# A recommendation tower on one core: three table looks replaced by six gathers, and a repack read over three queues

## The reference

```python
e = jnp.stack([tbl_0[ids[:, 0]], ..., tbl_25[ids[:, 25]]], axis=1)        # 2048 x 26 x 128
combined = jnp.concatenate([dense[:, None, :], e], axis=1)                # 27 features
interactions = jnp.einsum('bnd,bmd->bnm', combined, combined)[:, _TRIU_I, _TRIU_J]
h = jnp.concatenate([dense, interactions, dense], axis=1)
h = jnp.maximum(h @ W_top1 + b_top1, 0.0)                                 # 607 -> 512
h = jnp.maximum(h @ W_top2 + b_top2, 0.0)                                 # 512 -> 256
y = h @ W_top3                                                            # 256 -> 1
```

## Time and profile before

| | |
|---|---|
| median of 3 runs | 382.11 us (381.92 to 382.95) |
| profiled execution | 382.7 us, span 380.8 us |
| PE busy | 343.5 us, 90% |
| PEld busy | 306.4 us, 80% |
| POOL busy | 251.5 us, 66% |
| DVE busy | 193.3 us, 51% |
| ACT busy | 125.4 us, 33% |
| chain that ended last | PE 79%, DVE 12%, issue 4%, DMA 3%, ACT 1%, POOL 1% |
| DMA | 44.32 MB, mean 116 GB/s |

### The profile page before, as it was taken

The page is one execution under the profiler, slowest core; times in us unless marked ns, Lnnn a source line. Parts: engine busy times, 40 slices in busy tenths (PEclk is TensorE's granted clock), DMA queues, the critical chain, the costliest instruction groups (busy, mean ns, idle before and its releaser), DMA issues.

```text
span 380.8 us, 13111 instructions
## 1 busy us (share of the span) xinstructions
PE 343.5 (90%) x6048; PEld 306.4 (80%) x6048; DVE 193.3 (51%) x94; ACT 125.4 (33%) x211; POOL 251.5 (66%) x267
## 2 busy tenths in 40 slices
PE   0888878679999999999999999999999999999995
PEld 0878767579888898888988898889888898887763
DVE  3899995329733395228833395228733495200000
ACT  2343433214322342324322442324322343434122
POOL 4777887777777777777777777777777777600200
PEclk9999999759999999999999999999999999999999
DMA  8766534935522534235522535235522533331400
GB/s 207 166 177 167 137 93 142 278 104 183 131 76 58 189 91 124 58 86 173 134 72 53 194 84 131 58 112 152 134 63 59 188 88 79 125 93 29 158 8 0
DMA packets 31156, 44.32 MB, mean 116 GB/s; under 512 B 17659, under 2 KB 23043, under 8 KB 31102
## 3 DMA queue, kind: packets, MB, share of 16 engines
q1 hardware_dynamic: 22494, 26.44, 23.0%
q0 software_dynamic: 8320, 16.92, 17.3%
q10 hardware_dynamic: 288, 0.13, 0.2%
HBM read 32.97 MB, written 10.49 MB: 114 GB/s over the span
## 4 chain that ended last, share of the span: by engine, by line
PE 79%; DVE 12%; issue 4%; DMA 3%; ACT 1%; POOL 1%; SPq 0%; DVEq 0%
PE look_ps L317 34%; PE mid_ps L347 13%; PE layer_ps L364 11%; DVE match L472 9%; PE layer_ps L373 7%; PE mid_ps L329 7%; PE layer_ps L361 4%; DVE table_low L480 3%; DMA rows<-in_table,index 2%; PE layer_ps L380 2%; DMA look_ids<-in_look_rows 1%; POOL rows L298 1%; ACT hidden L539 0%; ACT hidden L545 0%; ACT turned L512 0%
## 5 line engine op out<-in xcount | busy, mean ns | idle before, releaser
L298 POOL DMA_INDIRECT rows<-in_table,index x256 | 248.3, 970 | 81.6 <-issue 75.6
L472 DVE TENSOR_TENSOR match<-look_ids,row_number_ps 125x2048 fp32r<-125x2048 int16 x80 | 181.8, 2285 | 129.3 <-PE look_ps L317 122.8
L317 PE MATMUL look_ps<-match,table_high 125*128 125x256 f32 x640 | 166.2, 297 | 19.3 <-DVE table_low L480 17.0
L317 PE MATMUL look_ps<-match,table_low 125*128 125x256 f32 x640 | 159.7, 287 | 2.9 <-issue 2.9
L317 PEld LDWEIGHTS look_ps<-match,table_high 125*128 125x128 f32 x640 | 124.8, 195 | 27.5 <-issue 18.1
L317 PEld LDWEIGHTS look_ps<-match,table_low 125*128 125x128 f32 x640 | 125.2, 196 | 0.0
L347 PEld LDWEIGHTS mid_ps<-turned 128*32 128x32 f32 x4096 | 46.8, 111 | 22.0 <-issue 19.0
L347 PE MATMUL mid_ps<-turned 128*32 128x27 f32 x4096 | 55.2, 198 | 8.8 <-issue 4.9
L512 ACT COPY turned<-look_ps 128x512 f32<-128x512 f32 x40 | 32.0, 799 | 74.8 <-PE look_ps L317 74.8
L364 PE MATMUL layer_ps<-pairs,w_pairs_sb 117*128 117x256 f32 x192 | 46.7, 378 | 0.0
L519 ACT COPY turned<-mid_ps 128x512 f32<-128x512 f32 x64 | 42.8, 672 | 11.3 <-PE mid_ps L329 10.8
(11 more groups left out here) (21 smaller groups left out, 44.8 us busy)
## 6 DMA issues: line engine op xcount, KB each, us to landing
scratch<-grams SPq DMA_DIRECT2D x8, 864.0 KB, 4.6
look_ids<-in_look_rows SPq DMA_DIRECT2D x40, 128.0 KB, 4.1
rows<-in_table,index POOLq DMA_INDIRECT x256
scratch<-grams SPq DMA_DIRECT2D x8, 416.0 KB, 5.8
pairs<-scratch SPq DMA_DIRECT2D x92, 29.2 KB
grams<-in_table SPq DMA_DIRECT2D x4, 448.0 KB
pairs<-in_table SPq DMA_DIRECT2D x3, 448.0 KB
hidden<-in_table SPq DMA_DIRECT2D x3, 448.0 KB
```

Source lines behind the costliest of these rows:

```text
L298: pool.indirect_dma_start(out=rows[j % 2][:, at, :], out_offset=None, in_=tables[GATHERED[at]], in_offset=bass.IndirectOffsetOnAxis(ap=ind ...
L317: last = nc.tensor.matmul(look_ps[pair % 2][:, r % 2, :], part[0:table_rows, r, c, :], match[number % 2][0:table_rows, c, :], start=(c == ...
L472: nc.vector.tensor_tensor(match[number % 2][0:table_rows], look_ids[b][0:table_rows, r % 2].unsqueeze(1).broadcast_to(shape), row_number_p ...
```

## The change

`EXTRA = (0, 1, 2)`: in these groups table 23, the tenth looked one, is not looked but gathered, into a tile of its own, `extra` (128 samples x 2 tiles x 128). `index` gets a 17th column with its ids.

- POOL issues two more gathers behind the 16 of tiles 0, 2 and 4. They wait for the whole index (first time) and for the last `turn_extra` (the others).
- PE has `turn_extra(g)`, two transposes into a `mid_ps` bank, in place of look(g, 9): behind look(0, 6) in group 0, behind turn(g, 3) in groups 1 and 2.
- The DVE makes no match for them. In the opening split_low(9) comes right behind split_low(8), in front of matches(1, 6) to (1, 8).
- ACT's copy of the fifth pair takes one look in those groups, and `take_extra` copies the two transposes.
- Numbers of looks, pairs and of the `mid_ps` steps come from lists written out in order.
- The last repack's middle chunk is issued by ACT, between relu1(6) and relu2(6), with a semaphore of its own.

```diff
+EXTRA = (0, 1, 2)
+COLUMNS = len(GATHERED) + 1
...
+        def looks_of(g):
+            return LOOKS - 1 if g in EXTRA else LOOKS
...
+        def mid_order():
+            yield from (("turn", 0, k) for k in range(5))
+            yield "extra", 0, 0
+            yield from (("turn", 0, k) for k in range(5, TURNS))
+            for g in range(1, groups):
+                for k in range(STEPS):
+                    yield "gram", g - 1, k
+                    yield "turn", g, k
+                if g in EXTRA:
+                    yield "extra", g, 0
+                if g + 1 < groups:
+                    yield from (("turn", g, k) for k in range(STEPS, TURNS))
...
-                for c in range(CHUNKS if g + 1 < groups else CHUNKS - 1):
+                for c in range(CHUNKS if g + 1 < groups else 1):
                     load_pairs(sp, g, c, pairs_in)
...
+                g = j // TILES
+                if j % TILES == 0 and g in EXTRA:
+                    if j == 0:
+                        pool.wait_ge(index_in, 16)
+                    after(pool, extra_turned, EXTRA.index(g))
+                    for t in range(TILES):
+                        pool.indirect_dma_start(
+                            out=extra[:, t, :], out_offset=None, in_=tables[LOOKED[LOOKS - 1]],
+                            in_offset=bass.IndirectOffsetOnAxis(ap=index[:, j + t, COLUMNS - 1:COLUMNS], axis=0),
+                        ).then_inc(extra_in, 16)
...
+            def turn_extra(g):
+                number = extra_number(g)
+                after(pe, mid_out, number - 2)
+                pe.wait_ge(extra_in, 16 * TILES * (EXTRA.index(g) + 1))
+                for t in range(TILES):
+                    last = nc.tensor.transpose(mid_ps[number % 3][:, t * P:(t + 1) * P], extra[:, t, :], identity[:])
+                last.then_inc(extra_turned, 1)
...
             look(0, 6)
+            turn_extra(0)
+            look(0, 7)
             turn(0, 5)
-            look(0, 7)
+            look(0, 8)
             turn(0, 6)
-            look(0, 8)
             turn(0, 7)
-            look(0, 9)
...
                 turn(g, 3)
-                look(g, 9)
+                if g in EXTRA:
+                    turn_extra(g)
+                else:
+                    look(g, 9)
...
-            for r in range(LOOKS):
+            for r in range(looks_of(0)):
                 matches(0, r)
                 split_low(r)
                 if r < AHEAD:
                     matches(1, r)
-            for r in range(AHEAD, LOOKS):
+            split_low(LOOKS - 1)
+            for r in range(AHEAD, looks_of(1)):
                 matches(1, r)
...
             for g in (groups - 2, groups - 1):
                 for half in range(2):
                     relu1(g, half)
+                if g + 2 == groups:
+                    act.wait_ge(scratch_in, SCRATCH_DMAS * groups)
+                    act.wait_ge(layer1_done, 2 * (groups - 2))
+                    load_pairs(act, groups - 1, 1, middle_chunk_in)
                 relu2(g)
                 copy_y(g)
```

More of the change, by code:

```diff
@@ L72, in build @@
         rows = [sbuf(f"rows{b}", [P, len(GATHERED), D]) for b in range(2)]
-        index = sbuf("index", [P, groups * TILES, len(GATHERED)], int32)
+        extra = sbuf("extra", [P, TILES, D])
+        index = sbuf("index", [P, groups * TILES, COLUMNS], int32)
         grams = sbuf("grams", [P, FEATURES, IN_QUAD])
@@ L109, in build @@
         gathered = [[sem(f"gathered{b}_{u}") for u in range(UNITS)] for b in range(2)]
+        extra_in = sem("extra_in")
+        extra_turned = sem("extra_turned")
         zeroed = sem("zeroed")
@@ L126, in build @@
         pairs_in = sem("pairs_in")
+        middle_chunk_in = sem("middle_chunk_in")
         last_chunk_in = sem("last_chunk_in")
@@ L142, in after, with look_order @@
                 eng.wait_ge(sem, count)
-        def look_number(g, r):
[L146 to L150, removed]
+        def looks_of(g):
+            return LOOKS - 1 if g in EXTRA else LOOKS
+        def look_order():
+            yield from ((g, r) for r in range(AHEAD) for g in (0, 1))
+            yield from ((g, r) for g in (0, 1) for r in range(AHEAD, looks_of(g)))
+            yield from ((g, r) for g in range(2, groups) for r in range(looks_of(g)))
+        look_place = {look: number for number, look in enumerate(look_order())}
+        def look_number(g, r):
+            return look_place[g, r]
         def pair_number(g, q):
@@ L157, in pair_number, with extra_number @@
             return LOOK_PAIRS * g + q
+        pair_place = {pair_number(g, q): (g, q) for g in range(groups) for q in range(LOOK_PAIRS)}
         def pair_end(number):
[L161 to L168, removed]
-        def turn_number(g, k):
[L171 to L176, removed]
+            g, q = pair_place[number]
+            return look_number(g, min(2 * q + 1, looks_of(g) - 1)) + 1
+        def mid_order():
[10 more added lines that the diff above has]
+                    yield from (("turn", g, k) for k in range(STEPS, TURNS))
+            yield from (("gram", g, 0), ("gram", g, 1))
+            yield from (("turn", g, k) for k in range(STEPS, TURNS))
+            yield from (("gram", g, 2), ("gram", g, 3))
+        mid_place = {step: number for number, step in enumerate(mid_order())}
+        def turn_number(g, k):
+            return mid_place["turn", g, k]
         def gram_number(g, k):
[L179 to L182, removed]
+            return mid_place["gram", g, k]
+        def extra_number(g):
+            return mid_place["extra", g, 0]
         block = ctx.enter_context(nc.Block())
@@ L498, in _ @@
             for g in range(2, groups):
-                for r in range(LOOKS):
+                for r in range(looks_of(g)):
                     matches(g, r)
@@ L511, in take_look, with take_extra @@
                 act.wait_ge(look_done, pair_end(number))
-                nc.scalar.copy(by_sample[g % 2][:, :, 1 + 2 * pair:3 + 2 * pair],
-                               look_ps[number % 2][:].rearrange("d f n -> d n f")).then_inc(looked, 1)
+                n = min(2, looks_of(g) - 2 * pair)
+                nc.scalar.copy(by_sample[g % 2][:, :, 1 + 2 * pair:1 + 2 * pair + n],
+                               look_ps[number % 2][:, 0:n].rearrange("d f n -> d n f")).then_inc(looked, 1)
+            def take_extra(g):
+                act.wait_ge(extra_turned, EXTRA.index(g) + 1)
+                nc.scalar.copy(by_sample[g % 2][:, :, LOOKS], mid_ps[extra_number(g) % 3][:, 0:N]).then_inc(mid_out, 1)
             def take_turned(g, k):
@@ L552, in copy_y @@
                 nc.scalar.copy(y_row[:, g % 2, :], layer_ps[1][0:1, 0, :]).then_inc(y_copied, 1)
-            nc.scalar.dma_start(index[:, 0], index_t[:, 0:len(GATHERED)]).then_inc(first_index_in, 16)
+            nc.scalar.dma_start(index[:, 0], index_t[:, 0:COLUMNS]).then_inc(first_index_in, 16)
             nc.scalar.dma_start(index[:, 1:].rearrange("p a b -> p (a b)"),
-                                index_t[:, len(GATHERED):]).then_inc(index_in, 16)
+                                index_t[:, COLUMNS:]).then_inc(index_in, 16)
             for r in range(RAWS):
@@ L566, in _ @@
             split_high(9)
+            take_extra(0)
+            take_look(0, 3)
             take_turned(0, 5)
-            take_look(0, 3)
             take_turned(0, 6)
+            take_look(0, 4)
             take_turned(0, 7)
-            take_look(0, 4)
             act.wait_ge(dense_in, 16)
@@ L594, in _ @@
                 take_turned(g, 3)
+                if g in EXTRA:
+                    take_extra(g)
                 take_look(g, 4)
@@ L659 @@
     w1_pairs = w1[order].reshape(CHUNKS, CHUNK_ROWS, H1).transpose(1, 0, 2)
-    index = a["ids"][:, GATHERED].reshape(batch // P, P, len(GATHERED)).transpose(1, 0, 2).reshape(P, -1)
+    index = a["ids"][:, GATHERED + LOOKED[-1:]].reshape(batch // P, P, COLUMNS).transpose(1, 0, 2).reshape(P, -1)
     low_halves = np.ascontiguousarray(a["ids"]).view(np.int16).reshape(batch, TABLES, -1)[:, :, 0]
```

5 lines of the change are left out of this document (3 added, 2 removed).

## The result

The changed kernel takes 385.05 us (median of 15 runs, 383.81 to 386.25) against 382.44 us for the kernel before beside it. The ratio is 1.0063 with a 95% interval of 1.0044 to 1.0082, so it is 1.7 to 3.1 us slower; 383.7 was forecast. One of the 15 executions of the kernel before took 639.39 us and is left out of the ratio. The profiled execution took 383.81 us, the fastest of the 15, with a span of 381.8 us (380.8 before). Its difference to the profile before, 1.1 us, is therefore smaller than that of the medians, 2.6 us.

What follows compares the result with a forecast made beforehand. POOL's gather row was taken as full, pinning a full PE: 2.8 us late at gather 64, 1.6 given back, 1.75 late at gather 96, hence +1.6: 384.3 us profiled, 383.7 median (own range 382.6 to 385.3; overall 381.3 to 387.0).

Steps and rivals of the forecast that it cites:

- Price of a look: On PE in groups 0 to 2: each look replaced by two transposes saves 1.6 us, 4.8 us in all if unhindered.
- Pin at gather 64: Last gather of group 1: its turn waits until 98.2 us against 95.46 before, so PE is 2.8 us late.
- Pin at gather 96: Last gather of group 2: its turn waits until 140.7 us against 138.95 before, 1.75 us late.
- Gather 40: In the opening: its turn at 65.7 us against 65.52 before, up to 71.0 if it meets the bulk load.
- The sum: Whole kernel: lateness from group 2 is carried to the end, +1.6 us, 384.3 us profiled, 383.7 for the median.
- Rival A: TensorE's clock falls in PE's new waits at gathers 40 and 64: +4.7 us, 386.8 us; chance 0.17.
- Rival B: Fewer opening gathers collide with DVE splits, each avoided moving both pins 0.75 us forward: 382.2 us or below; chance 0.15.
- Tail: Last repack's middle chunk moved from SP to ACT: 0 us, ends 0 and +0.8 us.
- T: Experiments' theory: POOL's full gather row pins PE at gathers 64, 96; gave extra_1 +0.4 us, extra_2 1.6 faster, extra_4_5 3.2 faster.

Runs made afterwards that it cites:

- gathers_beside: The kernel before with the six gathers added into a tile that nobody reads, all looks kept, old tail; ratio 1.0100 to the kernel before.
- no_gathers: The changed kernel with the old tail and without its six gathers, PE transposing zeros instead; ratio 0.9898 to the kernel before.
- gathers_old_tail: The changed kernel without its tail part, the last repack read over two queues again; ratio 1.0085 to the kernel before.
- tail_alone: The kernel before with only the tail part, ACT issuing the last repack's middle chunk; ratio 1.0018 to the kernel before.
- extra_1: The changed kernel with old tail and old opening order, table 23 gathered in group 1 alone; ratio 1.0057 to the kernel before.
- extra_2: The changed kernel with old tail and old opening order, table 23 gathered in group 2 alone; ratio 1.0001 to the kernel before.
- extra_4_5: The changed kernel with old tail and old opening order, table 23 gathered in groups 4 and 5; ratio 0.9998 to the kernel before.
- late_none: The kernel before with group 7's last four turns moved behind layer2(5), no gathers added; ratio 1.0076 to the kernel before.

## Why the prediction was right, and where it was off

The direction and the mechanism held. POOL's 66% was a full row. The six added gathers pushed its end from 330.48 to 337.09 us, which is 6 x 1.25 less one collision, and PE's saved looks turned into waits, among them those at the two gathers named. The chain runs through POOL up to gather 64, and gathers_beside and no_gathers show the same cost from both sides.

Not all of it held. The waits for rows came to 10.7 us where 3 to 8 were forecast, and the longest, 4.43 us at gather 52, is one for which the prediction listed no margin. It cost nothing of its own, because gather 64 pins PE behind it. The median lies 1.35 us above the forecast one, near the upper end of its own range (385.3), and the interval of the difference begins at 1.7 us, just above the forecast 1.6: the place was better predicted than the size.

- **Price of a look (1.6 us)**: 1.69 us in the profiles.
- **Pin at gather 64 (98.2 us)**: 98.97. The gather itself started at 94.84 in place of 95.7, a collision fewer, and its landing took 4.13 us to the turn, not 2.5. The two errors went against each other, which is luck. In gathers_old_tail the landing was 2.70.
- **Pin at gather 96 (140.7 us)**: 139.93, from 137.29 and a landing of 2.64.
- **Gather 40 (65.7 to 71.0 us)**: 69.07. It met the bulk load, as the upper end assumed; the turn of gather 64 made that lateness unimportant.
- **The sum (+1.6 us)**: +2.6 us in the medians, 1.7 to 3.1. In the profile PE was 1.0 us late at gather 96, 0.4 us early by group 6, and 1.0 us late at the end; in gathers_old_tail 1.3 us late at gather 96 and 2.2 at the last turn. That the profile ends as late as it was at gather 96 is luck too: PE had made the lateness good by group 6 and lost it again in group 7, in a pause of 0.73 us at 325.33 and in gram(7, 0), 2.16 us instead of 1.49. A term that the sum did not have is PE's own pauses, which I took as the same in both programs. They are not: they come at other places in each. No run shows how much of the missing 1 us they are.
- **Rival A (clock)**: its mechanism is there, but it does not set this profile's time. Time at 1.2 GHz is (1 - clock) x 2 x length: before 13.4 us in one stretch from 70 to 84; after 3.5 + 3.6 + 6.4 = 13.5 us in three pieces. Two of the three belong to waits for rows: behind the 3.20 us at gather 40 the clock was at 0.50 or 0.51 from 70 to 73 us, and in the 4.43 us at gather 52 it fell and stayed at 0.50 from 84 to 90. Both lie ahead of gather 64, where the chain is POOL's, so they delay nothing. The waits of 2.29 and 0.76 us at gathers 64 and 96 were not followed by a fall: from 98 to 141 us the granted clock was 1.00. In gathers_old_tail the wait of 2.47 us at the same gather 64 was, and cost 1.4 us. By the rule of the Trainium skill ("TensorE: Matmul & The Clock Gate", on oscillation in real kernels) waits for DMA bring repeated falls; the trace agrees at gathers 40 and 52 and shows none at 64 and 96. Over all 15 runs the mean granted clock of the changed kernel is 0.981, that of the kernel before beside the experiments 0.986 to 0.987. That is some 4 us more at 1.2 GHz, worth up to 2 us if all of it were on the path (an estimate from these means). gathers_beside is slower without it, so the clock is not needed for the effect; a share in the medians is not excluded.
- **Rival B (collisions)**: half right, and one collision is too few for it. With split_low(9) behind split_low(8) the gather at 51.53 took 1.79 us, as before, and the one at 54.87, where the last split had held a gather before, took 0.94: one collision gave 0.8 us back. I had argued that a merged collision would only last longer. The rule of the Trainium skill ("SBUF — State Buffer", who interferes with whom) that a DVE instruction with two SBUF inputs blocks a GpSimd read agrees with the trace here too, 1.79 us against 0.94, but my reading of it for two splits in a row does not: the two held one gather, and for no longer than one split had.
- **Tail (0)**: 0 by tail_alone's interval, which does not exclude a cost of 0.8 us. ACT's four loads took 3.8 us of its queue, from 359.62 to 363.38, longer than either end that I gave, and still ended ahead of relu2 at 364.21. The margin of PE against the last pairs, which I took as 1.1 us (363.9 against 365.04), comes and goes with the scratch's landing. SP's first load of pairs started 4.3 us behind the second scratch issue before and 6.0 after.

What stays open: why extra_1, extra_2 and extra_4_5 took 1.8, 1.6 and 3.1 us more than T gives, though the turns that T names stand within 0.5 us of its times. Each of the three profiles has a pause of about 1 us called issue in gram(7, 2) or gram(7, 3), which the profiles of before and after lack, but tail_alone, which is not slower than T gives, has one of 0.79 us there too; with one profile a kernel they are not shown to be the whole of it.

## What to carry to other kernels

An engine at 66% busy can be full: look at the idle pieces, and if all are the same 0.3 us of issue, count instructions by pitch instead. Before work is moved to such an engine, list for each consumer how long its data has been there, and charge every added instruction against the smallest margin behind it. Savings ahead of the tightest margin are lost, and savings behind it keep only what the next margin leaves. A sum made in this way gave the place and the sign here; late_none shows that a new order alone can cost as much as the change did.

## What the hardware showed that I had not expected

PE has pauses of 1 to 3.7 us that wait for nothing the profile shows. Most sit in grams, where 128 matmuls and their 128 weight loads go by in 1.5 us, and the longest under heavy DMA: 3.12 us at 71.43 in the earlier trace rows. What makes them no run shows. They move when PE's program changes its length or order, and in late_none a new order of the same instructions cost 2.9 us. A gather that started just behind a split took 0.7 to 1.0 us more, in 7 to 9 cases a profile: 1.98 us when it started 0.07 us behind the split, 1.78 at 0.26, 1.65 at 0.39, in place of 0.94. It seems to wait out the rest of the split's 1.22 us. The number changed from one kernel to the next. In late_none, with one more than before and no gather added, POOL's last gather started at 331.92 in place of 330.48, 1.4 us later.
